# Six stages on one core: stage three's moments, two normalisations and the clearing of its scratch rows move into stage two, and stage five's opening is put in another order

## The reference

```python
# stage three: the first layer's experts (8 of them, two for each token)
t = x * rsqrt(mean(x * x) + 1e-6) * norm_weight
gate_scores, expert_idx = top_k(t @ gate_w.T, 2)
w = softmax(gate_scores)
y = sum over the two chosen e of w_e * (gelu(t @ w1[e].T + b1[e]) @ w2[e].T + b2[e])

# stage five: the second layer's cross attention (16 heads of 64)
xn = layernorm(x) * gamma + beta
q, k, v = xn @ w_q, context @ w_k, context @ w_v
out = softmax(q k / sqrt(64)) v @ w_out + b_out
y = out * tanh(gate)
```

## Time and profile before

| what | value |
| --- | --- |
| median of three runs | 1596.78 us (1595.25 to 1599.88) |
| the profiled execution | 1611.02 us, its span 1609.1 us |
| PE / DVE / ACT / POOL busy | 90% / 58% / 52% / 41% |
| mean granted TensorE clock | 0.959 of full speed |
| bytes written to HBM | 58.21 MB |

### The profile page before, as it was taken

How to read it: one execution, slowest core, us unless ns; L and a number is a source line. 1 busy time by engine, 2 the same in 40 slices (tenths; PEclk the granted TensorE clock), 3 DMA queues, 4 the chain that set the end, 5 groups by cost and what they waited for, 6 DMA issues and landing times.

```text
span 1609.1 us, 38896 instructions
## 1 busy us (share of the span) xinstructions
PE 1445.7 (90%) x14805; PEld 1111.7 (69%) x14805; DVE 928.6 (58%) x2414; ACT 835.0 (52%) x1618; POOL 662.8 (41%) x678
## 2 busy tenths in 40 slices
PE   6999999996999997799778888549999999998997
PEld 5777776775777765579556666437888888885865
DVE  3344444346787746435688889536666667675223
ACT  4544555445776665246556666325555655543431
POOL 4243445424222115510588886323333444444034
PEclk9999999998999989799899999869999999999999
DMA  5021230000000520113000009920000000000323
GB/s 152 16 61 41 61 107 7 12 1 6 10 10 10 198 106 19 41 51 97 20 18 18 18 18 374 385 91 2 6 6 8 11 12 7 9 7 32 96 74 85
DMA packets 97824, 92.65 MB, mean 58 GB/s; under 512 B 21869, under 2 KB 71658, under 8 KB 97386
## 3 DMA queue, kind: packets, MB, share of 16 engines
q1 hardware_dynamic: 93034, 80.71, 15.5%
q0 software_dynamic: 4608, 9.45, 2.0%
HBM read 31.92 MB, written 58.21 MB: 56 GB/s over the span
## 4 chain that ended last, share of the span: by engine, by line
PE 59%; issue 14%; DVE 10%; POOL 7%; ACT 6%; DMA 1%; another core or an unknown queue 1%; SPq 1%; DVEq 0%; POOLq 0%; ACTq 0%
PE bank L2913 5%; PE bank L2945 5%; PE bank L1515 5%; PE bank L1499 4%; PE bank L2907 4%; PE bank L2924 4%; PE bank L2936 3%; PE bank L853 2%; PE bank L3566 2%; PE bank L873 2%; POOL s_p L1199 2%; PE bank L3555 2%; PE bank L826 2%; PE bank L2345 2%; PE bank L3557 2%
## 5 line engine op out<-in xcount | busy, mean ns | idle before, releaser
L1296 ACT COPY s_pT<-bank 77x512 f32<-77x512 f32 (+1 forms) x256 | 135.0, 584 | 110.0 <-PE bank L1499 109.8
L2735 POOL TENSOR_TENSOR s_p<-s_p,s_inverse 128x616 f32<-128x616 f32 x64 | 78.3, 1229 | 229.6 <-DVE s_inverse L2858 229.6
L1499 PE MATMUL bank<-ident,s_p 128*77 128x128 f32 (+1 forms) x1024 | 141.5, 285 | 14.5 <-ACT s_p L1289 10.6
L1499 PEld LDWEIGHTS bank<-ident,s_p 128*77 128x77 f32 (+1 forms) x1024 | 117.0, 148 | 43.8 <-ACT s_p L1289 23.5
L1199 POOL TENSOR_TENSOR s_p<-s_p,s_peak 128x1024 f32<-128x1024 f32 x64 | 120.2, 1900 | 27.5 <-DVE s_peak L1378 27.5
L1289 ACT ACTIVATE s_p<-s_p 128x616 f32<-128x616 f32 (+1 forms) x128 | 111.4, 891 | 18.9 <-POOL s_p L1199 14.4
L2842 DVE TENSOR_REDUCE s_peak<-bank 128x8 f32<-128x616 f32 x64 | 50.8, 794 | 88.3 <-PE bank L2924 88.3
L719 DVE TENSOR_TENSOR s_aT<-bank,s_weight 128x512 f32<-128x512 f32 x64 | 44.3, 692 | 98.7 <-PE bank L863 82.3
L1364 DVE TENSOR_TENSOR s_p<-bank,pos_bias 128x1024 f32<-128x1024 f32 x64 | 77.6, 1216 | 29.0 <-PE bank L1488 29.0
L1515 PE MATMUL bank<-s_pT,s_v 77*32 77x128 f32 (+1 forms) x2048 | 73.6, 287 | 21.5 <-DVE x_all L1404 20.4
L2913 PE MATMUL bank<-pos_bias,s_ctx 128*32 128x128 f32 x3072 | 91.4, 274 | 0.6 <-issue 0.6
(11 more groups left out here) (363 smaller groups left out, 3573.8 us busy)
## 6 DMA issues: line engine op xcount, KB each, us to landing
sorted_tokens<-s_zero SPq DMA_DIRECT2D x8, 4096.0 KB, 29.9
sorted_tokens<-s_zero SPq DMA_DIRECT2D x4, 2560.0 KB, 19.3
routed_tokens<-s_routed SPq DMA_DIRECT2D x24, 256.0 KB, 2.3
s_tokens<-sorted_tokens SPq DMA_DIRECT2D x48, 64.0 KB, 1.8
s_rows<-sorted_tokens SPq DMA_DIRECT2D x48, 64.0 KB, 1.8
x_all<-x SPq DMA_DIRECT2D x8, 256.0 KB, 3.1
w_s_gateup<-s_gateup SPq DMA_DIRECT2D x1, 2048.0 KB
out<-x_all SPq DMA_DIRECT2D x8, 256.0 KB
```

The lines of the kernel that those rows point to most:

```text
L1296: nc.scalar.copy(pT[0:keys, b % 2, 4 * q:4 * q + 4, :].rearrange("m h t -> m (h t)"), bank[0:keys, flip_bank("p", b, q), :]).then_inc(drai ...
L1499: last = nc.tensor.transpose(bank[0:keys, into, j * T:(j + 1) * T], p[:, b % 2, 4 * q + j, :], core.ident[:, :])
L2735: nc.gpsimd.tensor_tensor(part, part, inverse[:, b % 2, heads].unsqueeze(2).to_broadcast([P, HU, M]), ALU.mult).then_inc(share_ready, 1)
```

## The change

It does six things.

1. Stage three's moments (DVE) for groups 0 to 6 are taken in stage two, at every fourth step, and its scales (POOL) follow two steps later. Buffers for moments, scales, shifts and `kept` have a slot for each group. Group 7 comes at the start of stage three.
2. ACT normalises groups 0 and 3 in steps 28 and 30 of stage two.
3. The five sorted groups have token buffers of their own, and the dense groups share the sixth. `normalise` waits for no dispatch any more. `STARTS3` starts most groups one unit earlier (group 1 one later, group 4 two earlier).
4. The zeros are written in stage two, behind the context loads: both the rows of stage three and those that only stage six uses. After stage three's last quad only the lower 10.5 MB are cleared again.
5. Stage five opens with the keys' folds on PE, which don't wait for the gate. ACT copies them, four at once. Value folds and first keys come next, the flip of x after them.
6. The context loads of stage five wait for no memset; POOL's memset covers only the padding columns.

```diff
+            if following:
+                following.by_gpsimd(pool, b)
...
+            if following and step in (BATCH - 4, BATCH - 2):
+                following.by_scalar(act, (step - BATCH + 4) // 2)
...
-            if following and BATCH - 2 <= step < BATCH + 2:
-                following.by_vector(dve, step - BATCH + 3)
+            if following and step >= G + 3 and step % G == 3:
+                following.by_vector(dve, step // G - 1)
...
                     for g in range(1, GROUPS):
                         load_ctx(sp, g)
+                        if following and g >= 2:
+                            following.by_sync(sp, g)
...
-TOKENS = 6
+CLEARINGS_AT = {2: (0, 1), 3: (2, 3), 4: (4,), 5: (5,), 6: (6,), 7: (7,)}
+TOKENS = SORTED + 1
-STARTS3 = {3: 0, 1: 1, 4: 3, 5: 5, 6: 7, 7: 9, 2: 10}
+STARTS3 = {3: -1, 4: 1, 1: 2, 5: 4, 6: 6, 7: 8, 2: 10}
...
+    def clear_rows(sp, region, k, done):
+        count = (region.stop - region.start) // CLEARINGS3
+        piece = sorted_dram[region.start + k * count:region.start + (k + 1) * count, :]
...
-        for k in range(2):
-            sp.wait_ge(gathered[k], (SORTED + 1 - k) // 2 * G * 2 * 16)
-        cleared_rows = sorted_dram.rearrange("(k p j) d -> k p (j d)", p=P, k=CLEARINGS)
-        for k in range(CLEARINGS):
...
+        for k in range(CLEARINGS3):
+            clear_rows(sp, LOWER, k, regions_cleared)
...
         def normalise(g):
-            if i >= TOKENS:
-                earlier_g = ORDER3[i - TOKENS]
-                act.wait_ge(filled, turn["xnT", earlier_g] + 1)
-                if earlier_g >= DENSE:
-                    act.wait_ge(dispatched[earlier_g - DENSE], G * 2 * 16)
+            if 0 < g < DENSE:
+                act.wait_ge(filled, turn["xnT", g - 1] + 1)
...
-            sp.wait_ge(cleared, 2)
...
+            for k in range(2):
+                fold(k, w.s5_wkT, w.s5_wqT, keys_folded)
+            pe.wait_ge(wo_scaled, 1)
+            for k in range(2, 4):
+                fold(k, w.s5_wvT, w.s5_wo, values_folded)
+            pe.wait_ge(kq_ready, FOLDS)
             for h in range(H):
                 key_of(0, h)
+            flip_xn(0)
```

More of the change, by code:

```diff
@@ L1744, in stage3 @@
     gelu_ready = sem("gelu_ready")
-    dispatched = [sem(f"dispatched{j}") for j in range(SORTED)]
+    dispatched = sem("dispatched")
     rows_landed = [sem(f"rows_landed{k}") for k in range(FLIGHTS)]
@@ L1807, in hidden_at, with clear_regions @@
         return bank[:, HIDDEN + 2 * (q % 2) + n // 2, n % 2 * HID:(n % 2 + 1) * HID]
-    def by_sync(sp):
[L1810 to L1815, removed]
+    def clear_regions(sp, g):
+        sp.wait_ge(zero_ready, 1)
+        for k in CLEARINGS_AT[g]:
+            if k < CLEARINGS3:
+                clear_rows(sp, LOWER, k, cleared)
+            else:
+                clear_rows(sp, slice(E3 * REGION3, E6 * REGION), k - CLEARINGS3, regions_cleared)
+    LOWER = slice(0, E3 * REGION3)
+    def clear_rows(sp, region, k, done):
+        count = (region.stop - region.start) // CLEARINGS3
+        piece = sorted_dram[region.start + k * count:region.start + (k + 1) * count, :]
+        sp.dma_start(piece.rearrange("(p j) d -> p (j d)", p=P).rearrange("p (r c) -> p r c", c=GT),
+                     zero[:, :].unsqueeze(1).to_broadcast([P, count * D // P // GT, GT])).then_inc(done, 16)
+    def by_sync(sp):
         sp.wait_ge(gap_ready, 1)
@@ L1828, in by_sync @@
         sp.wait_ge(pairs_ready, 1)
[L1829 to L1832, removed]
+        sp.wait_ge(dispatched, SORTED * G * 2 * 16)
         for q in range(FLIGHTS):
@@ L2064, in by_scalar @@
                 gelu_of(k + 1)
[L2065 removed]
+            if group_in(k, 1) not in (None, ORDER3[1]):
                 normalise(group_in(k, 1))
@@ L2243, in by_vector @@
         if piece != "main":
-            if piece == 1:
-                before.x_of(dve, 0)
-                moments_of(0)
+            moments_of(piece)
             return
@@ L2687, in _ @@
[L2687 to L2700 removed]
+        FOLDS = 4
@@ L2715, in _ @@
         def _(pool):
+            x_from(pool)
+            pool.wait_ge(w.landed["s5"], w.count["s5"])
+            pool.wait_ge(w.landed["s6"], w.count["s6"])
+            nc.gpsimd.memset(ctx[:, :, :, M:MP], 0.0).then_inc(cleared, 1)
             def rstd_of(g, which):
@@ L2738, in _ @@
             rstd_of(0, 0)
+            nc.gpsimd.memset(p[:, :, :, :], 0.0).then_inc(cleared, 1)
+            route.constants_by_gpsimd()
             rstd_of(0, 1)
@@ L2895, in _, with fold @@
         def _(pe):
-            pe.wait_ge(fold_kept, H)
+            x_from(pe)
+            pe.wait_ge(w.landed["s5"], w.count["s5"])
+            pe.wait_ge(w.landed["s6"], w.count["s6"])
+            def fold(k, left, right, folded):
+                for pair in range(H // 4):
+                    for e in range(2):
+                        c, rows = H // 4 * k + pair, slice(DH5 * e, DH5 * (e + 1))
+                        last = nc.tensor.matmul(fold_bank(2 * k + e)[:, pair, :], left[rows, c % PAIRS, :],
+                                                right[rows, c % PAIRS, :], start=True, stop=True,
+                                                tile_position=(DH5 * e, 0))
+                        if pair == H // 4 - 1:
+                            last.then_inc(folded, 1)
             def flip_xn(g):
```

171 lines of the change are left out of this document (78 added, 93 removed).

## The result

The changed kernel takes 1552.56 us (median of 4 runs, 1544.24 to 1553.23) against 1598.33 of before: ratio 0.9706, 95% interval 0.9673 to 0.974. The forecast was 1556.3. The profiled execution took 1544.24 us (span 1542.4), 8.3 us less than its own median; the next fastest run took 1552.50.

What follows compares the result with a forecast made beforehand. PE is nearly nine tenths busy; the gain lies in its waits in stage three and from stage four to five. −20.8 − 12.2 − 12.5 + 5.0 = −40.5 takes the median 1596.8 to 1556.3 us; range 1540 to 1574.

Steps and rivals of the forecast that it cites:

- The three parts: Clearing at stage four's end, stage five's opening and own token buffers in stage three: −20.8, −12.2 and −12.5 us.
- the moves and turns: Moments, scales and normalising moved into stage two, charged 5 us (bounds 0 to 15); dispatches start one unit earlier.
- Clearing: End of stage four: the 20.79 us wait for zeros goes, as only 10.5 MB remain after stage three; gain 20.8 us.
- Late next is the addition to x: End of stage four: with the zeros done early, the last addition to x, at 1034.05, is what ends last.
- Opening: Stage five, first instruction to first scores: 30.2 us become 18.0, gain 12.2 us (bounds 5.5 to 15.6).
- The memset and DVE: Stage five's opening: the first norm waits out POOL's memset, 2.7 us later, changing nothing while keys are later.
- Token wait: Stage three: ACT's wait for a dispatch goes, with 8.6 us idle PE and 3.9 at low clock; gain 12.5, bounds 0 and 12.5.
- Stage two: Moments, scales and normalising added to stage two: DVE 1.5 us, ACT 3.4 us, POOL hidden; cost 5 us, bounds 0 to 15.
- Zeros in stage two: 33.5 MB of zeros beside stage two stop PE as often as before: 0, bounds −8.2 and +15 us.
- own sign of being wrong: Stage two shows gaps with no releaser followed by clock 0.50, or stage three still has a hole like that of 634.8.
- The hole at 670.8: Stage three, 670.8 to 682.4: 11.6 us with 2.73 us of PE work, left in both kernels as perhaps one execution's.
- the hole goes too: Rival, stage three: earlier dispatches remove the hole at 670.8, another 11.6 to 14 us, about 1543 us; chance 0.15.

Runs made afterwards that it cites:

- first series: Follow-up runs with before at 1596.59 us (13 runs): single parts, and three together, put into the kernel before; the changed kernel was not run in it.
- shared_tokens: Changed kernel with six shared token buffers and ACT's wait for group 3's dispatches again: 1571.36 us, against 1572.37 for the changed kernel.
- tokens_alone: Kernel before with only own token buffers for the sorted groups, order of turns as before: 1594.37 us, ratio 0.9977.
- third series: Follow-up runs with before at 1612.07 us (9 runs), including the changed kernel again at 1570.71 us.
- other two series: The second and third sets of follow-up runs, with before at 1609.63 and 1612.07 us; all their profiles show stops with "remote" waits.
- opening_alone: Kernel before with only stage five's new opening, zeros still at the end of stage four: 1585.14 us, ratio 0.9924.
- three_parts: Kernel before with clearing, own token buffers and stage five's opening; moments, scales, normalising and turns as before: 1562.43 us, ratio 0.9788; again 1573.23, 0.9776.

## Why the prediction was right, and where not

The total was right, 1556.3 against 1552.56, and a sum of −40.5 against −45.8, −37.3 and −41.4 us in the three pairs of medians. Its terms were not all right, and that the total came so near is in part luck: two errors cancelled. The three parts, forecast at −45.5, gave −34.2 in the first series and −38.8 in the third; the moves and turns, forecast at +5.0, gave about −10 and −2.5.

- **Clearing, −20.8:** −21.3 alone, the place and the size as said. "Late next is the addition to x": the chain shows it. In the changed kernel the last zeros start at 742.1, before stage four (forecast near 775).
- **Opening, −12.2:** −16.0 in the changed kernel's profile, −11.5 alone in the medians (14.2 us, below the forecast's bound of 14.6 at full clock; the gain is outside 5.5 to 15.6 by 0.4). The mechanism was right. The mis-sized terms: keys 10.26 against 8.53 (the row below has the clock at 1.00), scaling 1.29 against 0.76, values' folds 2.9 against 2.06, and the flip, which I put behind the keys with 1.08, came ready beside their copies. The bounds were also ill derived: with 8.5 or 16.4 us for the keys alone the recorded sum gives 16.2 and 24.1, not 14.6 and 24.7.

```profile
1008.20:1016.80 8.60, 8.60 (x37) 6.24 (x36) 8.01 (x21) 6.28 (x16) 4.36 (x8) 1.00 0.00 1
```

- **The memset and DVE:** the norm beside the memset took 3.46 us instead of 1.11, a delay of 2.4 us under cover of the keys, as the prediction said. The Trainium skill (SBUF — State Buffer, Who interferes with whom) has VectorE and GpSimd block each other at a shared pair of ports, for the whole of an instruction. The trace agrees: the first two of the four operations start at 1007.01 and 1007.27 and both end at 1009.9 to 1010.0, 0.3 us or so behind the memset's end at 1009.59, and the other two take 0.33 us each.
- **Token wait, −12.5:** wrong, −2.2 alone and nothing within the changed kernel (shared_tokens). The step that failed is "Late next in these units is PE itself. The dispatches start one unit earlier; only SP's tile loads wait for them, and PE comes to those after unit 23." Without the hole PE reaches its last dense unit at 113.7 us in tokens_alone, where SP issues the first load at 114.1: the loads are then what ends last, and PE waits 4.4 us for them.
- **Stage two, +5.0:** 1.7 us of it show. Of two normalisings one stops PE, for the 1.7 us forecast for each, and a group with DVE's moments in it still takes 23.20 us. The chain of the one that stops it reads:

```profile
543.04 1.65 ACT x_all L1977 x4
544.69 0.61 ACT s_p L1291
545.30 0.04 issue
545.35 0.66 PE bank L1503 x4
```

- What failed is the sentence behind it, "The units of stage three lose the same work, but PE was full there and gives nothing back": the row of dispatches ends 15 us earlier in the changed kernel's first profile (about 10 us in the medians), and the moves by themselves are −9.2 in the third series, net. In the first series' condition this and the token term are the same oversight with opposite sign: the sorted tiles' loads were never priced as a chain, from moments over 40 dispatches to SP. Beside the stops of the other two series that chain is not what ends last, and how the moves gain there stays open.
- **Zeros in stage two, 0 (−8.2 to +15):** stops of 2 us as in the earlier trace rows, one to three of them. The prediction's own sign of being wrong, a gap with no releaser and clock 0.50 behind it, did appear; it was a poor sign, as before has one too and the term allowed for as many. The one of the changed kernel cost about 3.8 us (2.0 and half of 3.5), where 8.2 were counted. Without most of the zeros the kernel was 6.6 us faster in one series and, with the old turns, 0.8 in the other. Within the bounds; PE in stage four is not slowed for the same data in the earlier trace rows, but 2.9 us appear there with the late zeros.
- **The hole at 670.8:** I let it stand in both kernels and took it for a thing of one execution. It is neither: it belongs to a condition that holds for a whole series. In the first series all four kernels without the moves are free of it, so its absence in the changed kernel's profile is no gain; before itself was not profiled there. opening_alone leaves stage three as it was, and its stage three takes 220.0 us against 229.2: about 9 of the 21 us by which the profiled difference exceeded the medians'. The rival "the hole goes too", with its 1543 us, is met by the one profiled execution of 1544.24 and by no other run.

## What to carry to other kernels

When a wait is removed, price the next thing with its own chain: a row of serial issues on a slow engine (40 dispatches, 1.26 us apart) that ends just before its result is wanted is the next bound. Look also whether it still is in another condition: in the first series the dense units ended 2 to 10 us behind the last dispatch, in the other two 14 to 21, and an earlier row bought nothing there. Undo a change part by part before explaining its sum: here two terms were wrong by 10 and about 15 us with opposite sign in the first series, and the total hid it. A single profile is not the median: the one read first here was the fastest run of its kernel. And check that two profiles come from the same condition, by a wait that the change can't touch, before subtracting them.

## What was not expected of the hardware

- Other engines than POOL stop beside a row of indirect dispatches in some series: ACT for up to 15.7 us with waits that name no releaser of the core, PE's matmuls 1.4 us apart in the hole of the earlier trace rows. The first series has none. The cause stays open; from 664 to 684 us in before's profile the only DMA packets are those of the dispatches themselves.
- Where a 16 KB instruction block came beside full DMA queues, PE stopped for 1.7 to 2.5 us at some blocks and not at all at most of them. The Trainium skill (Runtime: NRT & Kernel Launch, Instruction fetch mechanics) takes such fetches as mostly hidden; three_parts' stops at 467.1, 492.7 and 539.7 us say that beside full queues they may not be.
- Scaling 128x1024 by a column took 0.76 us at the new opening's start, with no memset beside it, and 1.29 in before, beside POOL's memsets.
